# A decoder layer on one core: another hand-written order of the middle stage, VectorE sums all output products before batch 1 is gated, turns of batches 1 and 2 stand between the up products

## What is computed

```python
x = x + attention(layernorm(x)) @ Wo + bo                 # 16 heads of 32, 2 key/value heads, causal
x = x + scan(ctx) * silu(layernorm(x))                    # selective state scan of ctx, gated by z
n = layernorm(x)
scores = sigmoid(n @ router_weight.T)                     # 16 experts, best 2 of the best 2 groups
routed = sum over the 2 chosen experts of weight * (relu(n @ w_up[e]) ** 2) @ w_down[e]
shared = (relu(n @ shared_up) ** 2) @ shared_down         # 512 -> 1024 -> 512
out = x + routed + shared
```

## Time and profile before

| | |
|---|---|
| median of 3 runs | 1271.38 us (1269.74 to 1272.44) |
| the profiled execution | 1268.8 us |
| its span | 1267.1 us |
| TensorE busy | 1079.4 us (85%) |
| VectorE busy | 805.8 us (64%) |
| ScalarE busy | 670.0 us (53%) |
| GpSimd busy | 672.2 us (53%) |
| mean granted TensorE clock | 0.966 |

### The profile page before, as it was taken

How to read it: one execution, slowest core, us unless ns; L and a number is a source line. 1 busy time by engine, 2 the same in 40 slices (tenths; PEclk the granted TensorE clock), 3 DMA queues, 4 the chain that set the end, 5 groups by cost and what they waited for, 6 DMA issues and landing times. The chain is left out here.

```text
span 1267.1 us, 18612 instructions
## 1 busy us (share of the span) xinstructions
PE 1079.4 (85%) x6368; PEld 643.5 (51%) x6368; DVE 805.8 (64%) x1195; ACT 670.0 (53%) x1440; POOL 672.2 (53%) x587
## 2 busy tenths in 40 slices
PE   7999748888888888888888995989999989999970
PEld 3444325555555555555555442444444446766740
DVE  5477689999999999999997466330580013233327
ACT  3566768888888888898887222201010112232220
POOL 1033379999999999999996700201040214445430
PEclk9999969999999999999999997989999999999995
DMA  6210001111111111122330302002107513344219
GB/s 199 85 35 18 18 18 34 35 35 34 34 35 34 35 30 31 34 51 76 101 84 9 134 34 100 34 27 73 67 2 243 170 35 121 127 129 129 77 53 371
DMA packets 51820, 94.74 MB, mean 75 GB/s; under 512 B 9806, under 2 KB 17998, under 8 KB 51728
## 3 DMA queue, kind: packets, MB, share of 16 engines
q1 hardware_dynamic: 44208, 72.82, 18.1%
q0 software_dynamic: 7520, 20.72, 5.3%
HBM read 74.51 MB, written 20.84 MB: 75 GB/s over the span
## 5 line engine op out<-in xcount | busy, mean ns | idle before, releaser
L604 POOL TENSOR_TENSOR w_all<-w_all 128x512 f32<-128x512 f32 x256 | 320.4, 1270 | 0.7 <-POOLq L96 0.3
L778 DVE TENSOR_TENSOR_SCAN w_all<-da,w_all 128x512 f32<-128x512 f32 x256 | 297.8, 1205 | 0.0
L712 ACT ACTIVATE da<-w_all,a_flat 128x512 f32<-128x512 f32 x256 | 179.4, 701 | 9.0 <-PEq L96 7.7
L683 PE MATMUL yb<-ident,w_all 128*128 128x128 f32 x1024 | 161.6, 281 | 7.5 <-DVE acc L786 7.5
L633 PE MATMUL sc<-w_all,attn 32*128 32x384 f32 (+3 forms) x512 | 105.0, 486 | 45.3 <-ACT w_all L720 22.8
L720 ACT ACTIVATE w_all<-sc,neg_max 128x128 f32<-128x128 f32 (+3 forms) x256 | 133.9, 539 | 16.6 <-DVE neg_max L770 15.6
L659 PE MATMUL ob<-w_all,v 128*32 128x128 f32 x1280 | 94.7, 277 | 52.6 <-ACT w_all L729 52.6
L1166 POOL TENSOR_TENSOR w_all<-w_all 128x512 f32<-128x512 f32 x24 | 29.1, 1212 | 195.0 <-ACT w_all L1335 195.0
L683 PEld LDWEIGHTS yb<-ident,w_all 128*128 128x128 f32 x1024 | 113.6, 141 | 37.0 <-issue 30.7
L770 DVE TENSOR_REDUCE neg_max<-sc 128x2 f32<-128x256 f32 (+3 forms) x128 | 104.1, 813 | 34.0 <-PE sc L636 34.0
L1227 PE MATMUL pc<-w_all 128*128 128x512 f32 x256 | 114.3, 603 | 12.9 <-DVE w_all L1375 12.9
(11 more groups left out here) (199 smaller groups left out, 1635.2 us busy)
## 6 DMA issues: line engine op xcount, KB each, us to landing
w_all<-b_scratch SPq DMA_DIRECT2D x64, 256.0 KB, 3.3
w_all<-in_w_up SPq DMA_DIRECT2D x16, 512.0 KB, 6.1
w_all<-in_w_down SPq DMA_DIRECT2D x16, 512.0 KB, 7.0
w_all<-sorted_y SPq DMA_DIRECT2D x16, 512.0 KB, 10.6
attn<-in_x SPq DMA_DIRECT2D x4, 1024.0 KB, 7.2
w_all<-in_x SPq DMA_DIRECT2D x16, 256.0 KB, 4.1
norms<-attn SPq DMA_DIRECT2D x4, 1024.0 KB, 4.3
out_dram<-acc SPq DMA_DIRECT2D x16, 256.0 KB, 8.3
```

What stands on the lines that cost most here:

```text
L604: pool.tensor_tensor(dbu[:, k, :], keep["du"][i // N][:, k * T:(k + 1) * T], b_all[i % 2][:, :], ALU.mult).then_inc(pool_dbu.sem, pool_dbu ...
L683: last = pe.transpose(yb[which][:, k * P:(k + 1) * P], state[i % 2][:, k, t * P:(t + 1) * P], ident[:, :])
L712: act.activation(da[unit % 2][:, :], keep["dt"][i // N][:, k * T:(k + 1) * T], ACT.Exp, scale=keep["a_flat"][:, unit % (N * KD):unit % (N ...
L778: dve.tensor_tensor_scan(state[i % 2][:, k, :], da[unit % 2][:, :], dbu[:, k, :], 0.0, ALU.mult, ALU.add).then_inc(dve_scan.sem, dve_scan. ...
```

## The change

No instruction is added or taken away, and none has another size. The lists of TensorE, ScalarE and VectorE in `close` have another order, and waits move with them:

- VectorE: `project_out` can be called for some of its row tiles, and its aggregates are a helper of their own, `aggregate(b)`. All sums of batches 2 and 3 now stand ahead of `gate(1)`. `logits(b)` is split into `copy_logits(b)` and `add_logits(b)`, and other calls stand between them. `gate(1)`, `normalize_n(1)`, `gate(2)`, `normalize_n(2)` follow each other.
- TensorE: `turn_z(1, ...)` moves from between the last output products to between the first `up` groups, and the turns of batches 2 and 3 move likewise. The one wait for the four sums of batch 3 ahead of `up(0, 0, 2)` becomes a wait for sum 0 ahead of group 0 and for sum 1 ahead of group 1, and the wait for sum 3 now stands ahead of `down(0, 0)`.
- ScalarE: `turned` copies two blocks per call, the roots and silu of batches 2 and 3 come ahead of nearly all of the `relu` calls.

```diff
@@ TensorE, up @@
                     if n >= 2:
                         pe.wait_ge(act_relu.sem, act_relu.upto(n - 2))
+                    else:
+                        pe.wait_ge(dve_x1.sem, dve_x1.upto(4 * LAST + n))
@@ TensorE, the list @@
             turn_n(0, 2)
-            turn_z(1, 0)
-            project_out(3, 2, 3)
-            turn_z(1, 2)
-            project_out(3, 3, 4)
+            project_out(3, 2, 4)
             pe.wait_ge(s_w_r.sem, s_w_r.upto(0))
             logits(0)
             pe.wait_ge(s_up_in.sem, s_up_in.upto(0))
-            pe.wait_ge(dve_x1.sem, dve_x1.upto(4 * LAST + 3))
             up(0, 0, 2)
             turn_logits(0)
+            turn_z(1, 0)
             up(0, 2, 3)
+            turn_z(1, 2)
+            up(0, 3, 5)
             turn_z(2, 0)
+            up(0, 5, 6)
             turn_n(1, 0)
-            up(0, 3, 4)
             turn_z(2, 2)
+            up(0, 6, 7)
             turn_n(1, 2)
-            up(0, 4, 6)
+            up(0, 7, 8)
             logits(1)
-            up(0, 6, 8)
             pe.wait_ge(s_down_in[0].sem, s_down_in[0].upto(0))
+            pe.wait_ge(dve_x1.sem, dve_x1.upto(4 * LAST + 3))
             down(0, 0)
             turn_logits(1)
+            turn_n(2, 0)
             turn_z(3, 0)
             down(0, 1)
+            turn_n(2, 2)
             turn_z(3, 2)
-            turn_n(2, 0)
             down(0, 2)
-            turn_n(2, 2)
+            logits(2)
             down(0, 3)
-            logits(2)
-            up(1, 0, 3)
+            up(1, 0, 2)
             turn_logits(2)
             turn_n(3, 0)
-            up(1, 3, 4)
+            up(1, 2, 3)
             turn_n(3, 2)
-            up(1, 4, 6)
+            up(1, 3, 5)
             logits(3)
-            up(1, 6, 8)
+            up(1, 5, 8)
             turn_logits(3)
@@ ScalarE, the list @@
             first_deviation(0)
             silu(0)
             first_deviation(1)
+            second_deviation(0)
+            turned(0, 0)
             silu(1)
-            second_deviation(0)
-            turned(0)
+            turned(0, 2)
             first_deviation(2)
+            first_deviation(3)
             silu(2)
+            relu(0, 0, 1)
+            silu(3)
+            relu(0, 1, 4)
             second_deviation(1)
-            first_deviation(3)
-            relu(0, 0, 2)
-            silu(3)
-            relu(0, 2, 4)
-            turned(1)
-            relu(0, 4, 5)
+            relu(0, 4, 6)
+            turned(1, 0)
+            relu(0, 6, 7)
+            turned(1, 2)
             second_deviation(2)
-            relu(0, 5, 8)
-            turned(2)
+            relu(0, 7, 8)
+            turned(2, 0)
+            turned(2, 2)
             second_deviation(3)
-            relu(1, 0, 4)
-            turned(3)
-            relu(1, 4, 8)
+            relu(1, 0, 2)
+            turned(3, 0)
+            relu(1, 2, 3)
+            turned(3, 2)
+            relu(1, 3, 8)
@@ VectorE, the list @@
-            project_out(0)
+            project_out(0, 0, 4)
+            aggregate(0)
             normalize_z(0)
-            project_out(1)
+            project_out(1, 0, 4)
+            aggregate(1)
             gate(0)
+            project_out(2, 0, 2)
+            normalize_n(0)
             normalize_z(1)
-            normalize_n(0)
-            project_out(2)
+            project_out(2, 2, 4)
+            aggregate(2)
+            project_out(3, 0, 4)
+            aggregate(3)
+            normalize_z(2)
+            copy_logits(0)
+            normalize_z(3)
+            add_logits(0)
             gate(1)
-            normalize_z(2)
             normalize_n(1)
-            project_out(3)
-            normalize_z(3)
-            logits(0)
             gate(2)
             normalize_n(2)
-            logits(1)
+            copy_logits(1)
+            add_logits(1)
+            base(0, 0)
             gate(3)
-            base(0, 0)
             base(0, 1)
             normalize_n(3)
-            logits(2)
             base(0, 2)
+            copy_logits(2)
             base(0, 3)
-            logits(3)
+            add_logits(2)
+            copy_logits(3)
+            add_logits(3)
             router.choose(dve)
```

More of the change, by code:

```diff
@@ L1322, in silu, with turned @@
                     act.activation(z[b][:, t, :], z[b][:, t, :], ACT.Silu).then_inc(act_silu.sem, act_silu.tick(4 * b + t))
-            def turned(b):
+            def turned(b, first):
                 act.wait_ge(dve_x2.sem, dve_x2.upto(4 * b + 3))
-                for k in four:
+                for k in (first, first + 1):
                     act.wait_ge(pe_nt.sem, pe_nt.upto(4 * b + k))
@@ L1369, in acc, with project_out @@
                 return keep["acc"][:, b, t * D:(t + 1) * D]
-            def project_out(b):
-                for t in four:
+            def project_out(b, first, end):
+                for t in range(first, end):
                     dve.wait_ge(pool_xb.sem, pool_xb.upto(4 * b + t))
@@ L1377, in project_out, with aggregate @@
                     dve.bn_stats(stats[0][b % 2][:, t, :], x1[b][:, t, :]).then_inc(dve_st1.sem, dve_st1.tick(4 * b + t))
+            def aggregate(b):
                 for t in four:
@@ L1413, in normalize_n, with copy_logits @@
                                       ALU.subtract, ALU.mult).then_inc(dve_n.sem, dve_n.tick(4 * b + t))
-            def logits(b):
+            def copy_logits(b):
                 dve.wait_ge(pe_lg.sem, pe_lg.upto(b))
@@ L1419, in logits, with add_logits @@
                 dve.tensor_copy(logit_t, bank[6][:, :]).then_inc(dve_lt.sem, dve_lt.tick(b))
+            def add_logits(b):
                 dve.wait_ge(pe_lt.sem, pe_lt.upto(b))
```

## The result

The changed kernel takes 1239.74 us (median of 4 runs, 1238.74 to 1240.67), the kernel before beside it 1271.53 us (1269.74 to 1272.44). The ratio is 0.9752, 95% interval 0.9735 to 0.9768, so the change is 31.8 us faster. The profiled execution took 1238.74 us with a span of 1236.9; the span of before was 1267.1.

A forecast was written before the change was run, and what follows sets the result against it. Middle stage bound by TensorE and VectorE waiting for each other in turn. Idle time 23.90 plus restarts 6.26 less waits 1.12 gave 29.0; midway to 29.7, 29.4: 1271.38 - 29.4 = 1242.0 us, range 1237.0 to 1251.0.

The forecast's parts named there:

- Idle time: TensorE's middle stage: six rows with 23.90 us of idle time ahead go; waits of 1.12 us stay or come.
- Restarts: Slow products behind the three long TensorE holes of the middle stage: 1.80, 2.22 and 2.24 us, together 6.26 us, go.
- From the other side: TensorE's own middle-stage work, 158.3 us, against 189.06: at most 30.8 us to gain, 29.7 less two waits.
- The two waits: TensorE's n turns of batches 2 and 3 wait for VectorE's addition of logits, 0.56 us each.
- the first sum: Middle stage: idle time and restarts removed, 30.16 us, less 1.12 us of waits, a gain of 29.0 us.
- The covers: TensorE work hiding other engines' chains: 9 us at first up, 2.6 at turn_n(1, 0), 1.1 at down(0, 3).
- rivals A and B: A: down(0, 3) waits behind gate(3), 1250.0 us, chance 0.12; B: turn_n(1) late, up to 1246.4 us, 0.09.
- Behind the stage: Router and expert loads count from TensorE's groups and move along, so the whole 29.4 us reaches the end.
- rival C: Gain swallowed if expert tiles wait for an unmoved transfer: 1271.4 us if wholly, 1256.7 if by half; chance 0.04.
- Rival D: Clock falls to 1.2 GHz under unbroken TensorE work; with 35 us of such work 1277.0 us; chance 0.03.
- The mark: Sign in TensorE's timeline: first down of batch 1 starts at 860 to 862 us; forecast wrong if behind 866.

The follow-up runs named there:

- the second trace of before: The kernel before, unchanged, run once more for its trace: 1269.95 us, stage 189.52 us.
- the version without any hole: Changed kernel, TensorE: turn_z(3, 0) ahead of turn_n(2, 0), and up(1, 2, 3) behind turn_logits(2): 1239.67 us, later 1240.20 us.
- with one call moved: Changed kernel with VectorE's base(0, 0) moved back behind gate(3): 1249.58 us.
- with 8 statistics: Changed kernel with 8 more VectorE statistics, results unused, between gate(3) and base(0, 1): 1243.06 us, one run.
- with 4: Changed kernel with 4 more VectorE statistics, results unused, between gate(3) and base(0, 1): 1240.71 us, one run.

## Why the prediction was right

The forecast was 1242.0 us with a gain of 29.4; measured are 1239.74 and a gain of 31.8 us, 29.6 of them in the stage of the two traces. That 29.4 and 29.6 lie so close is partly luck: the second trace of before would make it 30.1. By its steps:

- *Idle time.* 23.90 us were to go and 1.12 us to stay. The change has two holes of 0.56 us and no other. Right.
- *Restarts.* 6.26 us were to go, and no row of the stage is slow. Right, with the remark that this term isn't a constant: single restarts cost 1.70 to 3.13 us in these runs. The Trainium skill (TensorE: Matmul & The Clock Gate, section HAM oscillation) counts 26.7 us for 32 restarts, by which 0.83 us each would be an estimate. No trace here agrees: the smallest in the stage is 1.70.
- *From the other side.* 158.3 us of TensorE's own work were summed, and the version without any hole has a stage of 157.94. The two waits were put at 1.1 us and are 159.45 - 157.94 = 1.5: a hole is shown shorter by 0.17 us than what it costs, because the row ahead is drawn to its end (3.60 us) while the next could have started 3.43 us after it. The same small amount at four holes fewer, 0.7 us, is about the distance from the first sum, 29.0, to the measured 29.6.
- *The covers.* At the first `up` the wait for all four sums costs nothing, though the last of them is done only 0.13 us ahead; I had worked out only that sum 0 is covered by 9 us. At `turn_n(1, 0)` I had 2.6 us less up to 1.85 for GpSimd: VectorE's four tiles took 2.64 us instead of 1.92, from 779.78, and were done at 782.42, 1.8 us ahead of the turn at 784.21. At `down(0, 3)` the cover is 1.2 us. None ran out, so rivals A and B did not come.
- *Behind the stage.* 140.83 and 140.86 us to the expert tiles, so rival C, the swallowed gain, is refuted by the trace; the router's inverse is done at 915.21 and the product that reads it starts at 915.44, 0.23 us to spare as against 0.24. Rival D, a clock that falls under unbroken work, is refuted as well: granted clock 1.00 from 747 to 781 us and on to 930.
- *The mark.* The first `down` of batch 1 was to start at 860 to 862; it starts at 860.29.

What the prediction had not seen is how little the named parts of the order are worth by themselves. It said that VectorE's list holds late work in front of long-ready work, and took the sums as the case in point. The runs show that moving the sums alone loses 3.6 us of stage, and sums and logits together win 0.3, less than the 0.46 us between the two traces of before.

## What to carry to other kernels

When two engines run hand-written lists and one waits, name the first item in the other's list whose input is not there yet, not the item that is waited for: everything behind it is late, and moving one of those only lets the next one wait. Work out each cover as the time of what stands between on the waiting engine less the chain over the other engines, both from rows of the trace; that gave holes of 6.63 and 9.06 us and a cover of 1.2 us here to 0.2 us, and one of 16.97 us only to 1.3, with four tiles slowed beside GpSimd. And a stage whose start and end can be read from the profile settles differences that the medians of whole runs don't.

## What the runs showed of the hardware

- The cost of a restart of TensorE behind a hole varied between 1.70 and 3.13 us for the same 16 matmuls (7.03 or 7.13 us otherwise), behind holes of 3.52 and 6.63 us; behind the hole of 12.9 us it was 2.22, 2.53 and 2.67 in three traces, behind that of 5.76 us 2.09, 2.24, 2.39 and 2.90 in four. It doesn't follow the length of the hole. Only the restart behind the 3.00 us, at the output products, was 1.80 us in all five traces that have it. Behind 1.14 us nothing was slow.
- What a restart costs is the granted clock, to 0.1 us. Busy time by stretch while the `down` behind the hole ran, with one call moved (hole of 6.63 us), with 8 statistics (3.52) and with 4 (1.14):

```profile
822.19:832.18 9.99, 9.99 (x16) 4.04 (x16) 2.54 (x6) 0.00 (x0) 0.00 (x0) 0.69 0.28 105
```

```profile
825.53:834.19 8.66, 8.66 (x16) 3.74 (x17) 3.15 (x7) 0.00 (x0) 0.00 (x0) 0.80 0.33 123
```

```profile
823.51:830.48 6.97, 6.97 (x16) 3.15 (x17) 3.15 (x7) 0.00 (x0) 0.00 (x0) 1.00 0.41 153
```

The length of the stretch times what the clock lacks to 1.00 is 9.99 * 0.31 = 3.1, 8.66 * 0.20 = 1.7 and 0 us, and the restarts measured 3.13, 1.70 and none. Why the clock came back sooner in one than in the other, no run shows. With the sums and the logits moved it was 0.50 from the hole of 9.06 us on, through both slow turns and the hole of 1.80 us between them:

```profile
789.25:794.79 5.54, 3.73 (x17) 3.34 (x17) 3.88 (x10) 4.13 (x7) 0.00 (x0) 0.50 0.16 61
```

- Four VectorE tiles of tensor with two scalars, 1.92 us alone, took 2.64 us beside one of GpSimd's squares in the changed kernel, and 3.46 us in the kernel with the sums moved alone, beside two of them. Of that kernel, VectorE's timeline and GpSimd's:

```profile
786.69 3.46 DVE L1412 TENSOR_SCALAR attn<-acc,mean_var_c,rstd_c 128x512 f32<-128x512 f32 x4
```

```profile
787.20 2.22 POOL L1166 TENSOR_TENSOR w_all<-w_all 128x512 f32<-128x512 f32 x2 [62.61 <-ACT w_all L1335]
```

GpSimd's two squares took 2.22 us together; the one in the changed kernel took 1.36 us, where most take 1.04. A cover that is counted with 1.92 us should hold 3.8, what the earlier trace rows show beside GpSimd's sums. There the first of the four tiles alone took 2.40 of the 3.77 us.
